# Applying the attention in steps of 16 image rows, with the branch result loaded for two batches at once

## The reference

```python
attn = jax.nn.softmax(attn, axis=-1)
out = jnp.einsum('bhcd,bhdn->bhcn', attn, v).reshape(b, c, h, w)
out = jnp.einsum('bchw,oc->bohw', out, proj_w[:, :, 0, 0, 0])
return out + out_conv
```

## Time and profile before

| | us |
|---|---|
| median of 3 runs (6928.11 to 6961.05) | 6928.13 |
| the profiled execution, its own time | 6940.06 |
| its span | 6938.5 |
| `apply_attention`, first issue to last statistics (3761.1 to 4542.1) | 781.0 |
| PE busy in 3785 to 4540 | 578.2 |
| DVE busy in 3785 to 4540 | 480.3 |

### The profile page before, as it was taken

How to read it: one execution, slowest core, us unless ns; L and a number is a source line. 1 busy time by engine, 2 the same in 40 slices (tenths; PEclk the granted TensorE clock), 3 DMA queues, 4 the chain that set the end, 5 groups by cost and what they waited for, 6 DMA issues and landing times. The chain is left out here.

```text
span 6938.5 us, 79665 instructions
## 1 busy us (share of the span) xinstructions
PE 5361.6 (77%) x25018; PEld 2242.9 (32%) x25018; DVE 5420.2 (78%) x4182; ACT 3091.4 (45%) x3615; POOL 317.6 (5%) x492
## 2 busy tenths in 40 slices
PE   0999998999999576466665777769958887994887
PEld 0333333433333476233332222222212222221222
DVE  7223333999999799898995666669989996998998
ACT  0222222211111587255550000048857776885776
POOL 0111110000000000112120000000000000000000
PEclk9999999999999788678887787789978888997888
DMA  8666666999999996788887999946657764666775
GB/s 305 201 203 217 216 205 182 298 271 271 277 268 273 252 250 160 189 231 228 225 223 174 261 267 266 264 153 249 249 217 265 266 234 164 247 246 219 262 266 210
DMA packets 1173189, 1634.68 MB, mean 236 GB/s; under 512 B 82996, under 2 KB 903925, under 8 KB 1143285
## 3 DMA queue, kind: packets, MB, share of 16 engines
q1 hardware_dynamic: 834805, 1352.75, 63.6%
q10 hardware_dynamic: 314880, 201.39, 10.3%
q0 software_dynamic: 23424, 79.66, 4.5%
HBM read 975.88 MB, written 657.67 MB: 235 GB/s over the span
## 5 line engine op out<-in xcount | busy, mean ns | idle before, releaser
L544 PE MATMUL dw_p<-dw_it,dw_tt 128*128 128x512 f32 x2304 | 1027.8, 607 | 114.5 <-DVE dw_tt L460 81.5
L583 DVE SCALAR_TENSOR_TENSOR dw_vo<-dw_vi,keep_wv,dw_vo 128x2048 f32<-128x2048 f32 x384 | 903.1, 2352 | 13.6
L909 PE MATMUL bc_p<-bc_z,bc_wc 128*32 128x256 f32 x9216 | 571.3, 413 | 350.6 <-DVE bc_z L951 350.6
L951 DVE STREAM_TRANSPOSE bc_z<-bc_xp 96x1536 f32<-96x1536 f32 (+1 forms) x256 | 718.3, 2912 | 98.1 <-DMA bc_xp<-d 95.1
L1160 PE MATMUL ap_p<-ap_vt,ap_pw 96*96 96x512 f32 x1024 | 588.5, 740 | 190.2 <-DMA ap_xt<-in_x 185.3
L345 PE MATMUL pw_p<-pw_xh,pw_wlo 128*128 128x512 f32 x1280 | 586.2, 605 | 185.1 <-POOL pw_xh L298 185.1
L544 PEld LDWEIGHTS dw_p<-dw_it,dw_tt 128*128 128x128 f32 x2304 | 442.5, 194 | 699.9 <-issue 667.3
L561 ACT ACTIVATE dw_ot<-dw_p 128x512 f32<-128x512 f32 x384 | 216.4, 599 | 925.7 <-PE dw_p L544 661.1
L909 PEld LDWEIGHTS bc_p<-bc_z,bc_wc 128*32 128x32 f32 x9216 | 322.5, 119 | 599.5 <-issue 436.2
L1537 DVE TENSOR_TENSOR_SCAN wb_sums<-wb_ewt,wb_fb 128x3078 f32<-128x3078 f32 x64 | 424.3, 6630 | 2.3
L1797 DVE TENSOR_TENSOR_SCAN wf_sums<-wf_ewt,wf_fb 128x3078 f32<-128x3078 f32 x64 | 424.3, 6630 | 2.3
(11 more groups left out here) (323 smaller groups left out, 9145.3 us busy)
## 6 DMA issues: line engine op xcount, KB each, us to landing
u<-pw_ut SPq DMA_DIRECT2D x64, 2048.0 KB, 8.2
dw_it<-u SPq DMA_DIRECT2D x192, 512.0 KB, 10.9
d<-dw_ot ACTq DMA_DIRECT2D x192, 512.0 KB, 12.3
gr_qk<-d SPq DMA_DIRECT2D x128, 768.0 KB, 9.2
bb_d<-wb_bb SPq DMA_DIRECT2D x64, 1536.0 KB, 5.2
wf_bb<-bb_d SPq DMA_DIRECT2D x64, 1536.0 KB, 7.5
bc_xp<-d SPq DMA_DIRECT2D x216, 288.0 KB, 10.1
bc_xp<-d POOLq DMA_DIRECT2D x192, 288.0 KB, 9.2
```

The source lines that it names most:

```text
L544: mm = nc.tensor.matmul(po[c][:, :].rearrange("p (b w) -> p b w", b=B), tt[:, h, 3 * c + dx, 0:H], it[:, h, B * c:B * (c + 1), dx:dx + W], ...
L583: nc.vector.scalar_tensor_tensor(vo[:, h], src, w, vo[:, h], ALU.mult, ALU.add).then_inc(tapped, 1)
L909: mm = nc.tensor.matmul(po[q % NBANK][32 * c4:32 * c4 + 32, :, :], wc[:, c, dx, :, :].rearrange("p j r -> p (j r)"), z[:, h, c, :, dx:dx + ...
L951: last = nc.vector.transpose(z[rows, h, :, b % 2, 1 + S * k:1 + S * k + S], xp[rows, b % 2, k, :, :].rearrange("p s c -> p c s"))
```

## The change

T becomes 2048, which is 16 image rows: 32 steps in place of 64, each with 8 products where there were 4. The tiles `vt`, `xt` and `xo` double, and a row of their transfers is 8 KB. There are still 4 PSUM banks, so a product now shares its bank with another of its own step.

`tt` is organised otherwise. One half now holds a pair of batches (b = 0, 1 or b = 2, 3) for all 16 rows, and is loaded by 24 transfers of 128 KB whose rows in device memory are 1 KB: the two batches lie beside each other there. The half of a pair is loaded again, for piece j + 1, when the pair's second batch has read it. DVE reads `tt` with a pattern of 4 rows of 128 points, 1 KB apart.

```diff
-    T, SUB = 1024, 512
+    T, SUB = 2048, 512
+    NQ = T // SUB
+    NT = 2 * NQ
+    NBANK = 4
+    RT = T // W
+    RB = 8
-    NLT = C // 16
+    NLT = C // 16 * (RT // RB)
...
-        tt = st.sb("tt", [HALF, 2, 2, T])
+        tt = st.sb("tt", [HALF, 2, 2, RT, 2, W])
...
-        tv = t.rearrange("j g (p r) (q b w) -> b (j g) q p r w", r=8, b=2, w=W)
+        tv = t.rearrange("j g (p r) (q b w) -> (j g) q p r (b w)", r=RB, b=2, w=W)
...
-        def load_t(act, j, b):
-            for q in range(C // 16):
-                m, p = divmod(16 * q, HALF)
-                src = tv[b % 2, bass.ds(2 * j + b // 2, 1), q].rearrange("a p r w -> (a p) r w")
-                act.dma_start(tt[p:p + 16, b % 2, m, :].rearrange("p (r w) -> p r w", w=W), src).then_inc(t_loaded[b % 2], 16)
+        def load_t(act, j, h):
+            for k in range(RT // RB):
+                for q in range(C // 16):
+                    m, p = divmod(16 * q, HALF)
+                    src = tv[bass.ds(2 * (RT // RB * j + k) + h, 1), q].rearrange("a p r n -> (a p) r n")
+                    act.dma_start(tt[p:p + 16, h, m, RB * k:RB * k + RB, :, :].rearrange("p r b w -> p r (b w)"),
+                                  src).then_inc(t_loaded[h], 16)
...
-                        sp.wait_ge(added, 4 * (4 * j + b + 2))
+                        sp.wait_ge(added, NT * (4 * j + b + 1) + NBANK)
...
-                                mm = nc.tensor.matmul(po[2 * q + m][:, :], pw[:, b, k, m * HALF:(m + 1) * HALF],
+                                mm = nc.tensor.matmul(po[(2 * q + m) % NBANK][:, :], pw[:, b, k, m * HALF:(m + 1) * HALF],
...
-                    dve.wait_ge(t_loaded[b % 2], 16 * NLT * (2 * j + b // 2 + 1))
+                    dve.wait_ge(t_loaded[b // 2], 16 * NLT * (j + 1))
...
-                            nc.vector.tensor_tensor(xo[:, b % 2, m, cols], po[2 * q + m][:, :], tt[:, b % 2, m, cols],
-                                                    ALU.add).then_inc(joined, 1)
+                            nc.vector.tensor_tensor(by_row(xo[:, b % 2, m, cols]), by_row(po[(2 * q + m) % NBANK][:, :]),
+                                                    tt[:, b // 2, m, rows, b % 2, :], ALU.add).then_inc(joined, 1)
...
-                        act.wait_ge(joined, 4 * (4 * j + b + 2))
-                        own_wait(act, passed)
-                        load_t(act, j if b < 2 else j + 1, (b + 2) % B)
+                for h in range(2):
+                    act.wait_ge(joined, NT * (4 * j + 2 * h + 2) + NBANK)
+                    own_wait(act, passed)
+                    load_t(act, j + 1, h)
```

More of the change, by code:

```diff
@@ L1094, in apply_attention @@
         ss = st.sb("ss", [HALF, B * 2, 2])
-        po = [st.ps(f"p{k}", [HALF, SUB]) for k in range(4)]
+        po = [st.ps(f"p{k}", [HALF, SUB]) for k in range(NBANK)]
         pgm = st.ps("pgm", [HALF, B * 4])
@@ L1155, in _ @@
                     pe.wait_ge(loaded[b % 2], 32 * (2 * j + b // 2 + 1))
-                    for q in range(2):
+                    for q in range(NQ):
                         for m in range(2):
-                            pe.wait_ge(joined, 4 * n + 2 * q + m + 1)
+                            pe.wait_ge(joined, NT * n + 2 * q + m + 1)
                             for k in range(2):
-                                mm = nc.tensor.matmul(po[2 * q + m][:, :], pw[:, b, k, m * HALF:(m + 1) * HALF],
+                                mm = nc.tensor.matmul(po[(2 * q + m) % NBANK][:, :], pw[:, b, k, m * HALF:(m + 1) * HALF],
                                                       vt[:, b % 2, k, q * SUB:(q + 1) * SUB], start=k == 0, stop=k == 1)
@@ L1180, in _ @@
         def _(dve):
-            dve.sem_inc(added, 4)
-            dve.sem_inc(joined, 4)
+            dve.sem_inc(added, NBANK)
+            dve.sem_inc(joined, NBANK)
             with dve.Fori(0, NJ) as j:
@@ L1186, in _ @@
                     dve.wait_ge(loaded[b % 2], 32 * (2 * j + b // 2 + 1))
-                    dve.wait_ge(t_loaded[b % 2], 16 * NLT * (2 * j + b // 2 + 1))
+                    dve.wait_ge(t_loaded[b // 2], 16 * NLT * (j + 1))
                     dve.wait_ge(stored[b % 2], 16 * (2 * j + b // 2) + 1)
-                    for q in range(2):
+                    for q in range(NQ):
                         for m in range(2):
                             cols = slice(q * SUB, (q + 1) * SUB)
-                            dve.wait_ge(product, 4 * n + 2 * q + m + 1)
-                            nc.vector.tensor_tensor(xo[:, b % 2, m, cols], po[2 * q + m][:, :], tt[:, b % 2, m, cols],
-                                                    ALU.add).then_inc(joined, 1)
-                    for q in range(2):
+                            rows = slice(q * SUB // W, (q + 1) * SUB // W)
+                            dve.wait_ge(product, NT * n + 2 * q + m + 1)
+                            nc.vector.tensor_tensor(by_row(xo[:, b % 2, m, cols]), by_row(po[(2 * q + m) % NBANK][:, :]),
+                                                    tt[:, b // 2, m, rows, b % 2, :], ALU.add).then_inc(joined, 1)
+                    for q in range(NQ):
                         for m in range(2):
                             cols = slice(q * SUB, (q + 1) * SUB)
-                            dve.wait_ge(joined, 4 * n + 2 * q + m + 5)
+                            dve.wait_ge(joined, NT * n + 2 * q + m + NBANK + 1)
                             nc.vector.tensor_tensor(xo[:, b % 2, m, cols], xo[:, b % 2, m, cols], xt[:, b % 2, m, cols],
                                                     ALU.add).then_inc(added, 1)
-                    dve.wait_ge(added, 4 * (n + 2))
-                    for q in range(2):
+                    dve.wait_ge(added, NT * (n + 1) + NBANK)
+                    for q in range(NQ):
                         for m in range(2):
-                            last = nc.vector.bn_stats(bn[:, 2 * b + m, bass.ds(12 * j + 6 * q, 6)],
+                            last = nc.vector.bn_stats(bn[:, 2 * b + m, bass.ds(6 * NQ * j + 6 * q, 6)],
                                                       xo[:, b % 2, m, q * SUB:(q + 1) * SUB])
@@ L1231, in _ @@
             load_t(act, 0, 1)
-            def turn(j, last):
-                for b in range(B):
-                    if not (last and b >= 2):
-                        act.wait_ge(joined, 4 * (4 * j + b + 2))
-                        own_wait(act, passed)
-                        load_t(act, j if b < 2 else j + 1, (b + 2) % B)
             with act.Fori(0, NJ - 1) as j:
-                turn(j, False)
-            turn(NJ - 1, True)
+                for h in range(2):
+                    act.wait_ge(joined, NT * (4 * j + 2 * h + 2) + NBANK)
+                    own_wait(act, passed)
+                    load_t(act, j + 1, h)
             act.wait_ge(avg, 4)
```

## The result

The changed kernel takes 7011.52 us (median of 4 runs, 7000.11 to 7030.73) and the kernel before, on the same chip, 6941.24 (4 runs, 6928.11 to 6961.05). The ratio is 1.0102, interval 1.0061 to 1.0142: it is slower by 1.0%. The prediction had 6892 and a range of 6830 to 6945, and its likeliest case was faster.

A forecast was written before the change was run, and what follows sets the result against it. It took a full transfer queue as the stage's bound, the two-buffer loop closing as well. Start 48, third step 35, 29 steps x 2w and end 24 gave 745 us against 781.0: kernel 6892, range 6830 to 6945.

The forecast's parts named there:

- likeliest case: Whole kernel: gains come as summed, w 10.6 to 11.3, stage 722 to 762, kernel 6869 to 6909; chance 0.52.
- tt's wait: DVE's wait for tt, late in 39 steps: reload now covered by 17 us; worth nothing while the queue is full.
- Account 1: Transfers of one unit (1024 points, one batch): reads 7.6, store 2.2, q10 alone 1.9; 11.7 us against 11.84.
- tt's transfers: Rows of 1 KB on q10 instead of 512 bytes: saves 0.1 to 1.0 us a unit, 0.5 taken.
- Rival 2: tt's time goes by bytes or landing place, only 0.1 saved; stage 768 or 794; sign q10 under 320 packets/us; chance 0.19.
- Rival 3: q1's longer rows read faster, 0.25 to 0.29 MB/us; stage 687, -94 us, or -110; chance 0.17.
- Rival 4: Slower by four PSUM banks for eight products and PE's clock: w 12.8, +68 us, kernel 6996; chance 0.12.
- w: Time of one unit, 1024 points of one batch, in the stage's steady part: 11.84 us before, 11.0 forecast.
- The pauses: q1's slow restart after idle, 166 GB/s against 260, loses 0.7 us a step; halved steps save 0.35 us a unit.
- The start: Stage's first issue to DVE's beginning: 22.9 us before, 48 us forecast.
- the third step: Third step of the stage: begins some 35 us after DVE's beginning.
- The end: Last step of the stage, from its first L1193: 12 us before, 24 us forecast.

The follow-up runs named there:

- the spreading: Changed kernel with each tt transfer sent to 16 partitions six apart instead of 16 neighbours (branch result added to other channels): 6976.44 us, 1.0049, stage 806.1.

## Why the prediction was wrong, point by point

**The step that failed** is "tt's wait": "Now 24 take 17.5 us, 27 with the landing, against the two steps of the other pair, 44 us: covered by 17 us", and with it "This is worth nothing by itself while the queue is full, so it is not in the sum". The two steps are about as predicted (42 us, 3895 to 3937), but tt took 79. Of this the issues took 49 in place of 17.5, since ACT's issues themselves had to wait, and the rest of the load came in behind them. The 9.4 us of the earlier trace rows were a landing beside q1's packets of 4 KB. The prediction itself had that q10 moves packet for packet with q1, and that q1's packets are halved in number; it used both for how much is left over, and not for how fast a load comes in. The cut back to 4 KB showed what that costs: 58 of 62 us.

**Account 1 adds up only while there is always something to send.** With tt late in large lumps, v and x are both loaded, SP has nothing to issue until DVE has added, and then the engines run dry: 0.35 us a unit that no term held.

**tt's transfers**, "I take the middle, 0.5" saved. Rival 2's sign of it came: q10 alone does 218 packets of 1 KB a us, under 320. The rate by bytes even fell, 0.198 and 0.177 MB/us against 0.229. So the saving did not come: q10 alone took 1.15 us a unit before and 2.13 after, 0.98 more where the sum had 0.5 less. 0.42 MB a unit were left after, near the 0.49 of the sum, but only 0.26 before, where it had 0.50. The 0.26 shows that more rides than one packet for each of q1's: over the us in which q1 reads and q10 moves too, q10 moved 141 packets a us before and 47 after. One for one holds where q1 is busy throughout, and was too hard for the mean. So the 11.7 of account 1 met the measured 11.84 by luck: q1 moved in 10.70 us a unit and not in 9.8, q10 alone in 1.15 and not in 1.9.

**The rivals.** Rival 2 had the right doubt on tt, but its time, 768 to 794, lacked the starving. Rival 3 is refuted: rows of 8 KB read no faster. Rival 4's figure, 6996 with w = 12.8, is near the result, and its cause is wrong: the PE steps of 32 matmuls in the rows around took 15.9 to 17.2 us, PE was busy 545 us and not longer, and without tt the long steps were 34 us better with the same four banks. PE did wait for banks, but because DVE waited for tt.

**The pauses.** The 166 GB/s of the earlier trace rows were misread. This is q1 and q10 together, and q10 moved 0.24 of the 0.33 MB in those two us, so the pause was not lost, and account 1 had it already as time of q10 alone. Before, there is no us in which neither moves. In the scan q1 moves in 0.53 us a unit less, where 0.35 was forecast, but with less of tt riding along at the same time: that the pauses gave it is not shown. Without tt the steady unit falls by 1.2 us, over the bound of 0.7.

**What held.** The start: 51.3 us for 48, the third step 40.7 behind for 35. The end: 18.4 for 24, since PE has four products ready when the last step begins. The pattern of 4 x 128 on DVE cost nothing: L1201 takes 682 ns, 685 before.

In the terms of w: q10 alone +0.98 where -0.5 was summed, neither queue +0.35 where nothing was, q1 -0.53 where -0.35 was; together 1.65 above the 11.0 of the sum. Sum of the misses: start +3.3, third step +5.7, steady part 58 x 1.64 = +95, end -5.6; together 98, which is 843.4 - 745. The range was too narrow since none of its cases had a late tt.

**Open.** Why q10 alone is slower with longer rows, and slower still with long steps and the old tt, is not settled; where the bytes land is a part of it in the changed kernel, by the spreading (0.198 to 0.224). Why long steps with the old tt took 911.6 us is not explained by the packet count alone. Why pairs in short steps lose 32 us with tt never late is argued, not shown.

## What to carry to other kernels

When two queues share the transfer engines, a transfer's landing time belongs to the other queue's packet size: before lengthening one queue's rows, divide its rate by the new row length, and ask whether the small-packet queue can still bring its load in by that many packets a us. A buffer loaded in larger lumps must be priced by that rate, not by its issues, and a late lump stops the other queue as well, since that one waits for the buffers to come free. If longer steps are wanted for the loop's sake, keep the transfers cut at the old row length: here that gave back most of what was lost, though it gained nothing over the short steps. Shortening the rows further, to 2 KB, gave nothing in the short steps and lost 36 us in the long ones. A rate read in a pause of one queue must be split by queue first: what the other one moves in it is not lost.

## What the runs showed of the hardware that was not expected

- Rows of 1 KB into 16 partitions were not faster alone than rows of 512 bytes: 0.198 and 0.177 MB/us against 0.229.
- Both queues move nearly equal numbers of rows while q1 reads, whether its rows are of 2, 4 or 8 KB: 103 beside 107, 53 beside 55, 26 beside 27 a us (medians; kernel before with rows of 2 KB, kernel before, changed kernel).
- 16 partitions six apart in place of 16 side by side shortened the stage by 37 and 25 us, at the same bytes and rows.
- ACT's issues can block. An issue takes 0.57 us in the median, but where tt landed late a single one took 11.2 us, and the longest of the stage 13.9 us (durations min/median/max in ns, first and last start in us):

```profile
L1125 ACTq DMA_DIRECT2D ap_tt<-t x384: 567/572/13912, 3759.7 to 4530.3; - x192
```
